# A two-layer gated cross-attention kernel: output weights split inside the first attention, semaphores cleared by runs, and a reordered merged stage

## The chip, the cores and the metric

The kernel runs on one core of a Trainium2 chip. The metric is the device time in microseconds (us) of one execution. A core has five engines that run their own programs and wait for each other by semaphores: PE (TensorE, matmuls; PEld is its weight load), DVE (VectorE), ACT (ScalarE), POOL (GpSimd) and SP (SyncE, which issues most transfers here).

## The reference

`x` is 2048 tokens of 512 numbers, `ctx_2048` as many. Two layers follow each other, and each adds two gated parts to `x`:

```
x = x + tanh(g_xattn[0]) * L0_xattn(layernorm(x), ctx)     # 16 heads of 128; in groups of 128 tokens
x = x + tanh(g_ffn[0])   * L0_ffn(layernorm(x))            # 8 experts, the best 2 of each token, and a shared one
x = x + tanh(g_xattn[1]) * L1_xattn(layernorm(x), ctx)     # 16 heads of 32; per token, over its own heads
x = x + tanh(g_ffn[1])   * L1_ffn(layernorm(x))            # weights rounded to -1, 0, 1 times their mean magnitude

L0_xattn: q, k = rms_norm(x @ q_w + q_b), rms_norm(ctx @ ki_w + ki_b); v = ctx @ vi_w + vi_b
          softmax(q k^T / sqrt(128)) v, then @ o_w + o_b
L1_xattn: Q, K, V = x @ Wq.T + bq, ctx @ Wk.T + bk, ctx @ Wv.T + bv
          score = einsum('bshd,bsgd->bshg', Q, K); softmax over g; einsum('bshg,bsgd->bshd') @ Wo.T + bo
```

## The kernel before

**Stages.** Four stages run one after the other: `l0_attention`, `l0_experts`, `l1_attention` (called the merged stage: it adds the experts' rows to x, and does the second attention) and `l1_output_ffn`. `build` wraps each in a call of `stage`: after the stage's own programs it clears on POOL, one instruction for one semaphore, the semaphores of the stage before it, and then meets all engines at a barrier. After the last stage the last semaphores are cleared in the same way.

**Precision.** Every 32-bit operand of a matmul is split in two: a high part (rounded to PE's fp32r by ACT, functions `..._high_part`) and a low part (operand minus high part, by POOL or DVE, `..._low_part`, `w_low`, `c_low`). A product takes three passes (`PASSES`), so 12 matmuls of 512 columns fill one 128x512 tile from a depth of 512.

**`l0_attention`.** The 2048 tokens go in four blocks of 512, each with 4 tiles of 128 tokens; the first three blocks are a hardware loop, the fourth is written out. A block takes 16 weight groups of 1 MB (`i` from 0 to 15) through two slots, `i % 2`: 4 for k, 1 for v, 4 for q, 3 more for v, and 4 for the output (from `O0` = 12). For each group SP loads (`load_w`), ACT rounds (`w_high_part`), POOL subtracts (`w_low`, one instruction of 128x2048), PE multiplies (`project`, `project_out`), and DVE takes the results (`take`). Beside groups 0 to 3 a tile of x is loaded (`load_x`), normalised on DVE and POOL (`normalise_x`), turned on PE (`turn_h`) and split (`h_high_part`, `h_low_part`). On each engine the written order is the order of execution. DVE's program for group `i` is: normalise tile `i`, then take the four results of group `i`. Inside group 11 all engines run `attention`: 16 units `u` of four heads and 128 tokens, scores, maximum, exponent, sum (`L631`) and reciprocal (`L633`), product on POOL (`L301`), turning with a lag of 3 units and weighing with a lag of 4. From unit 10 on ACT and DVE also split the first four heads for the output projection (`a_high_part`, `a_low_part`, `L612`). The weights of group 13 (the second of the output) are split after the attention. At a block's end DVE adds the bias to four residual tiles (`L664`), SP stores them (`L232`), and then loads x of the next block (`L202`).

**`l1_attention`.** Again four blocks `b` of 512 tokens. Its projections come as items (kind, block, tile): `h` turns a tile of normalised x, `k`, `v`, `q` are projections of 12 matmuls. The items of block 0 and `k` of block 1 come first, alone. Then 32 pairs `p` follow, 8 to a block (`w = p % 8`); each does a part of the attention of block `b` and holds two items of the next block, or of `k` of the block after that, in its two slots. Results of q, k, v are stored in DRAM and loaded again in another layout (`store`, `load_q`, `load_k`, `load_v`); ACT's `move_queries` lays q out before a block's first scores. In pairs 4 and 5 of blocks 0 and 1 the context of two blocks later is rounded (`c_high_part`) and subtracted (`c_low`), and in pairs 4 to 7 a tile of it is normalised (`tile_stats`, `power`, `tile_normalise`), whose expert rows POOL gathers (`gather`) two tiles ahead. The magnitudes of the last stage's weights are summed in 32 pieces (`sum_piece`, loads by `load_piece`), two in each of the last 16 pairs.

## Time and profile before

| what | us |
|---|---|
| median of 3 timed runs | 2105.95 (2105.8 to 2112.45) |
| the profiled execution, its device time | 2103.36 |
| the profiled execution, its span from the first to the last instruction | 2101.6 |
| PE busy in the span | 1928.2 (92%) |

The trace is of one execution. Its device time is 1.8 us more than its span. TensorE's mean granted clock is 0.966 of full speed. "Busy" of PE counts a matmul's modelled length, so it says where PE waited, and not that it was at its peak where it did not.

### The profile page before, as it was taken

To read this page: it belongs to the slowest core of one execution; us is meant where nothing else is said; L and a number is where in the kernel's file an instruction comes from. 1 tells how busy PE (TensorE), PEld (TensorE's weight loads), DVE (VectorE), ACT (ScalarE), POOL (GpSimd) and SP (SyncE) were. 2 spreads that over 40 slices of the span, in tenths; PEclk is the share of its full clock that TensorE was granted. 3 is DMA by queue.
4 is the path that set the end of the run, shared out by engine and by line. 5 is a ranking of instruction groups with operands and counts; after the bars stand their busy time and mean duration, and the time that the engine had idled before them with its cause. 6 is when DMAs were issued, how large, how long until landed. Compare 5 with 4: busy or idle time off the path is not lost. (4 is left out here: it accounts for less than half of the span.)

```text
span 2101.6 us, 29461 instructions
## 1 busy us (share of the span) xinstructions
PE 1928.2 (92%) x10300; PEld 1613.6 (77%) x10300; DVE 1039.0 (49%) x1659; ACT 749.7 (36%) x1128; POOL 1076.1 (51%) x807
## 2 busy tenths in 40 slices
PE   6999999999999999979999799998789875899997
PEld 5888788877897788857777699996677763678885
DVE  2547654765565655663341233334677764782111
ACT  3326333633345333622122112223333444443332
POOL 5765477547844775443227846523354323843332
PEclk9999999999999999989999899998999986999998
DMA  4231332224221322243217655423966555430000
GB/s 146 101 110 34 133 105 90 71 76 134 92 95 66 122 99 100 102 172 120 105 59 265 195 169 173 144 71 116 289 155 181 152 156 165 156 110 31 20 20 20
DMA packets 172236, 248.11 MB, mean 118 GB/s; under 512 B 44944, under 2 KB 69520, under 8 KB 172112
## 3 DMA queue, kind: packets, MB, share of 16 engines
q1 hardware_dynamic: 157024, 202.09, 30.7%
q0 software_dynamic: 9472, 34.09, 4.8%
q10 hardware_dynamic: 5616, 10.23, 1.3%
q8 instruction: 85, 1.39, 0.3%
q14 instruction: 39, 0.32, 0.1%
HBM read 179.77 MB, written 66.58 MB: 117 GB/s over the span
## 5 line engine op out<-in xcount | busy, mean ns | idle before, releaser
L255 POOL TENSOR_TENSOR a_w_hl<-a_w_raw,a_w_hl 128x2048 fp32r<-128x2048 f32 x63 | 290.7, 4615 | 150.8 <-ACT a_w_hl L320 150.8
L436 PE MATMUL a_proj<-a_c_hl,a_w_hl 128*128 128x512 f32 x768 | 183.0, 398 | 21.4 <-DVE a_w_hl L556 19.9
L436 PEld LDWEIGHTS a_proj<-a_c_hl,a_w_hl 128*128 128x128 f32 x768 | 146.1, 192 | 53.4 <-issue 20.3
L510 PE MATMUL a_proj<-a_w_hl,a_a_hl 128*128 128x512 f32 x768 | 179.5, 392 | 4.0 <-DVE a_a_hl L612 4.0
L436 PE MATMUL a_proj<-a_w_hl,a_c_hl 128*128 128x512 f32 x768 | 181.2, 392 | 0.0
L436 PE MATMUL a_proj<-a_a_hl,a_w_hl 128*128 128x512 f32 x768 | 176.4, 390 | 0.0
L320 ACT ACTIVATE a_w_hl<-a_w_raw 128x2048 fp32r<-128x2048 f32 x64 | 122.4, 1912 | 151.1 <-PE a_proj L436 106.7
L339 ACT ACTIVATE a_sq<-a_proj,a_vecs 128x512 f32<-128x512 f32 x128 | 88.0, 690 | 230.9 <-PE a_proj L436 153.4
L510 PEld LDWEIGHTS a_proj<-a_w_hl,a_a_hl 128*128 128x128 f32 x768 | 142.7, 188 | 34.3 <-POOL a_w_hl L255 5.5
L436 PEld LDWEIGHTS a_proj<-a_a_hl,a_w_hl 128*128 128x128 f32 x768 | 143.6, 188 | 29.7
L279 POOL TENSOR_TENSOR a_ssum<-a_ssum,a_sq 128x512 f32<-128x512 f32 x112 | 145.4, 1298 | 37.1 <-ACT a_sq L339 32.4
L436 PEld LDWEIGHTS a_proj<-a_w_hl,a_c_hl 128*128 128x128 f32 x768 | 142.4, 188 | 28.6
L1293 PE MATMUL b_gate_up<-b_wts,b_xt_hl 128*128 x936 | 159.8, 326 | 4.2 <-DVE b_xt_hl L1502 4.2
L2499 POOL TENSOR_TENSOR f_a_hl<-f_act_sb,f_a_hl 128x512 fp32r<-128x512 f32 x64 | 86.8, 1358 | 146.7 <-ACT f_a_hl L2547 146.6
L1293 PEld LDWEIGHTS b_gate_up<-b_wts,b_xt_hl 128*128 128x128 f32 x936 | 154.9, 191 | 8.2 <-issue 5.0
L612 DVE SCALAR_TENSOR_TENSOR a_a_hl<-a_qT,a_vecs,a_a_hl 128x512 fp32r<-128x512 f32 x64 | 101.1, 1609 | 81.7 <-ACT a_a_hl L353 81.7
L1199 PE MATMUL b_gate_up<-b_wts 128*128 128x512 f32 (+1 forms) x576 | 136.0, 394 | 0.0
L1896 POOL TENSOR_TENSOR p_probs<-p_own_sc,p_mask 128x512 f32<-128x512 f32 x64 | 67.8, 1082 | 128.9 <-DVE p_own_sc L2237 128.6
L1199 PEld LDWEIGHTS b_gate_up<-b_wts 128*128 128x128 f32 (+1 forms) x576 | 102.9, 179 | 29.4
L2607 PE MATMUL f_totals<-f_ternary,f_a_hl 128*128 128x512 f32 x512 | 122.6, 396 | 0.3 <-DVE f_ternary L2631 0.3
L2593 PE MATMUL f_hidden<-f_h_hl,f_ternary 128*128 x512 | 118.8, 389 | 0.0
L2607 PEld LDWEIGHTS f_totals<-f_ternary,f_a_hl 128*128 128x128 f32 x512 | 96.3, 188 | 23.9 <-issue 0.8
(254 smaller groups left out, 3522.7 us busy)
## 6 DMA issues: line engine op xcount, KB each, us to landing
a_w_raw<-in_a_ki_w SPq DMA_DIRECT2D x16, 1024.0 KB, 5.0
a_w_raw<-in_a_vi_w SPq DMA_DIRECT2D x16, 1024.0 KB, 4.9
a_w_raw<-in_a_q_w SPq DMA_DIRECT2D x16, 1024.0 KB, 4.9
a_w_raw<-in_a_o_w SPq DMA_DIRECT2D x16, 1024.0 KB, 5.3
spare<-in_b_gate_up POOLq DMA_DIRECT2D x32, 352.0 KB, 3.8
l_sorted_rows<-b_zeros SPq DMA_DIRECT2D x39, 256.0 KB, 3.2
spare<-l_sorted_rows SPq DMA_DIRECT2D x39, 256.0 KB, 3.2
l_expert_out<-spare ACTq DMA_DIRECT2D x39, 256.0 KB, 3.5
```

What stands on the lines that cost most here:

```text
L255: pool.tensor_tensor(w_hl[:, s, 1], w_raw[:, s], f32(w_hl[:, s, 0]), ALU.subtract)\
L279: pool.tensor_tensor(ssum[:], first, sq[:, n % 2, :], ALU.add).then_inc(sq_added, 1)
L320: act.activation(w_hl[:, i % 2, 0], w_raw[:, i % 2], ACT.Copy).then_inc(w_high, 1)
L339: act.activation(sq[:, n % 2, :], proj[:, j, :], ACT.Square, bias=bias)\
L436: mm = pe.matmul(proj[:, j, :], left, right, start=(k == 0 and n == 0), stop=(k == KC - 1 and n == 2))
L510: mm = pe.matmul(proj[:, j, :], a_hl[:, ap, k, j * P:(j + 1) * P], w_hl[:, i % 2, wp, k], start=(n == 0 and m == 0), stop=(n == 4 * G - 1 ...
L612: dve.scalar_tensor_tensor(a_hl[:, 1, n % 4, :], qT[:, n, :], v_b[:, n:n + 1], f32(a_hl[:, 0, n % 4, :]), ALU.add, ALU.subtract).then_inc( ...
L1199: mm = pe.matmul(gu_ps[0:w, n, part, :], gu_hl[:, s, wp, k, cols], h_hl[:, hslot, ap, k, :], start=(k == 0 and m == 0), stop=(k == KC - 1 ...
L1293: mm = pe.matmul(gu_ps[:, i % 2, half, 0:F], x_part(i, xp)[:, own], part(r, P, at, F), start=(k == 0 and xp == 0 and start == HI), stop=(k ...
L2499: pool.tensor_tensor(a_hl[:, 1, m % FC, :], act_sb[:, m % 2, :], f32(a_hl[:, 0, m % FC, :]), ALU.subtract).then_inc(g_split, 1)
L2593: mm = pe.matmul(h_ps[:, m % 2, :], w_t[:, 2 * g, k, f * P:(f + 1) * P], h_hl[:, ap, k, bass.ds(BLK * t, BLK)], start=(k == 0 and ap == 0) ...
L2607: mm = pe.matmul(y_ps[:, j, :], a_hl[:, ap, f, j * P:(j + 1) * P], w_t[:, 2 * g + 1, f, :], start=(m == 0 and ap == 0), stop=(m == NG * FC ...
```

## The change

Three parts of the program change.

1. In `l0_attention`, POOL's subtraction of a weight group is four instructions of 128x512 in place of one of 128x2048, everywhere. Group 13 is split inside the attention: ACT rounds a quarter in units 4, 5, 6 and 8 (`O_HIGH`), POOL subtracts a quarter in units 9, 10, 12 and 13 (`O_LOW`). Two of the four early `a_low_part` go behind the attention's loop. Tile 0 of x is turned and split together with tile 1, after group 1, and SP loads tiles 2 and 3 one group later.
2. In `build`, semaphores with numbers next to each other are cleared by one instruction.
3. In `l1_attention`, the expert rows of the first four tiles are gathered at once, two of them into buffers that are free until later; POOL subtracts the q weights and DVE the v weights (it was the other way round); `take_v` comes earlier in DVE's program; q is loaded before v in block 0. In the pairs, ACT's two roundings and POOL's two subtractions of the context come first in the pair. For the last block the items are h, h | h, h | q, q | q, q | v | v | v | v over the 8 pairs (they were h, v four times, then q, q twice, then none). The pieces are summed from pair 0 on, one in a pair (two in pairs 22 to 25), all on ACT, and are done after pair 27.

The diff, cut to its core:

```diff
+    O_HIGH, O_LOW = (4, 5, 6, 8), (9, 10, 12, 13)
...
-                    if i < 2:
-                        load_x(i + 2)
+                    if 0 < i < 3:
+                        load_x(i + 1)
...
             def w_low(n, i):
                 pool.wait_ge(w_high, n + 1)
                 s = i % 2
-                pool.tensor_tensor(w_hl[:, s, 1], w_raw[:, s], f32(w_hl[:, s, 0]), ALU.subtract)\
-                    .then_inc(w_split, 1)
+                for k in range(KC):
+                    ins = pool.tensor_tensor(w_hl[:, s, 1, k], w_raw[:, s, k], f32(w_hl[:, s, 0, k]), ALU.subtract)
+                ins.then_inc(w_split, 1)
...
                             if u % 4 == 3 and not last:
                                 c_low(KC * t + KC, u // 4)
-                        w_low(NW * t + i + 2, i + 2)
+                            if u in O_LOW:
+                                w_low_part(NW * t + i + 2, i + 2, O_LOW.index(u))
...
+                            if u in O_HIGH:
+                                act.wait_ge(proj_ready, NP * t + NP)
+                                w_high_quarter(NW // 2 * t + (O0 + 1) // 2 + 1, O0 + 1, O_HIGH.index(u))
...
-                    if i == O0:
-                        w_high_part(NW // 2 * t + (i + 1) // 2 + 1, (i + 1) % 2)
...
                     project(i)
-                    if i < TPB:
-                        turn_h(i)
+                    if 0 < i < TPB:
+                        for j in range(0 if i == 1 else i, i + 1):
+                            turn_h(j)
...
-                        if EARLY < u <= EARLY + 4:
+                        if EARLY < u <= EARLY + 2:
                             a_low_part(u - EARLY - 1)
+                    for n in (2, 3):
+                        a_low_part(n)
...
+    SLOTS = []
     for n in range(1, NBLK):
-        ITEMS += [(kind, n, j) for j in range(4) for kind in "hv"] + four("q", n)
+        pairs = list(zip(four("h", n), four("v", n)))
         if n + 1 < NBLK:
-            ITEMS += four("k", n + 1)
-    NI = len(ITEMS)
+            pairs += list(zip(four("q", n)[::2], four("q", n)[1::2])) + list(zip(four("k", n + 1)[::2], four("k", n + 1)[1::2]))
+        else:
+            pairs = list(zip(four("h", n)[::2], four("h", n)[1::2])) + list(zip(four("q", n)[::2], four("q", n)[1::2]))
+            pairs += [(item, None) for item in four("v", n)]
...
-        PIECES = []
-        for p in range(2 * NP, NP * NBLK):
-            PIECES += [(p, "act"), (p, "dve")] if p in (2 * NP + 4, 2 * NP + 5) else [(p, "act")] * 2
+        PIECES = [(p, "act") for p in range(28) for _ in range(2 if 22 <= p < 26 else 1)]
...
-            load_v(0)
             for j in range(TPB):
                 store("q", 0, j)
             load_q(0)
+            load_v(0)
...
+                if b + 2 < NBLK and w in (4, 5):
+                    c_low(b + 2, 2 * w - 8)
+                    c_low(b + 2, 2 * w - 7)
                 if p:
                     expand(2 * p - 2)
                     expand(2 * p - 1)
...
             tile_stats(0)
-            w_low("q", 0)
             tile_stats(1)
-            w_low("q", 1)
             tile_normalise(0)
-            tile_stats(2)
-            w_low("q", 2)
-            tile_normalise(1)
             dve.wait_ge(const_in, 32)
             take_v(0, 0)
+            tile_stats(2)
+            tile_normalise(1)
             take_v(0, 1)
...
+    def clear(sems):
+
+        numbers = sorted(s.num for s in sems)
+        first = [n for n in numbers if n - 1 not in numbers]
+        after = [n + 1 for n in numbers if n + 1 not in numbers]
+        for start, stop in zip(first, after):
+            nc.gpsimd.sem_clear(range(start, stop))
```

The order on PE at a block's start in `l0_attention` (written-out order of the first block; `a_proj` is the projection of a group, `a_turned` a turned tile of x). Before:

```order
L436 MATMUL a_proj<-a_c_hl,a_w_hl 128x512 x12
L445 MATMUL a_turned<-a_ident,a_xr 128x128 x4
L418 REGISTER_ALU
L430 ISA
L436 MATMUL a_proj<-a_c_hl,a_w_hl 128x512 x12
```

After:

```order
L455 MATMUL a_proj<-a_c_hl,a_w_hl 128x512 x12
L437 REGISTER_ALU
L449 ISA
L455 MATMUL a_proj<-a_c_hl,a_w_hl 128x512 x12
L449 REGISTER_ALU
L455 MATMUL a_proj<-a_c_hl,a_w_hl 128x512 x12
L449 REGISTER_ALU
L455 MATMUL a_proj<-a_c_hl,a_w_hl 128x512 x12
L449 REGISTER_ALU
L455 MATMUL a_proj<-a_c_hl,a_w_hl 128x512 x12
L464 MATMUL a_turned<-a_ident,a_xr 128x128 x8
```

Nothing stands between the last tile of group 0 and the first of group 1 any more, and both turned tiles come after group 1.

The order on POOL ahead of the attention, in it and behind it (`a_rq` is the reciprocal root for q, `a_probs` is the product of unit u, `a_c_hl` the context's subtraction, `a_w_hl` that of the weights), in the last block. Before:

```order
L255 TENSOR_TENSOR a_w_hl<-a_w_raw,a_w_hl 128x2048
L283 TENSOR_TENSOR a_rq<-a_rq,a_mhalf 128x4
L255 TENSOR_TENSOR a_w_hl<-a_w_raw,a_w_hl 128x2048 x2
L301 TENSOR_TENSOR a_probs<-a_probs,a_rden 128x512 x16
L255 TENSOR_TENSOR a_w_hl<-a_w_raw,a_w_hl 128x2048 x3
```

After:

```order
L292 TENSOR_TENSOR a_rq<-a_rq,a_mhalf 128x4
L257 TENSOR_TENSOR a_w_hl<-a_w_raw,a_w_hl 128x512 x8
L310 TENSOR_TENSOR a_probs<-a_probs,a_rden 128x512 x10
L263 TENSOR_TENSOR a_w_hl<-a_w_raw,a_w_hl 128x512
L310 TENSOR_TENSOR a_probs<-a_probs,a_rden 128x512
L263 TENSOR_TENSOR a_w_hl<-a_w_raw,a_w_hl 128x512
L310 TENSOR_TENSOR a_probs<-a_probs,a_rden 128x512 x2
L263 TENSOR_TENSOR a_w_hl<-a_w_raw,a_w_hl 128x512
L310 TENSOR_TENSOR a_probs<-a_probs,a_rden 128x512
L263 TENSOR_TENSOR a_w_hl<-a_w_raw,a_w_hl 128x512
L310 TENSOR_TENSOR a_probs<-a_probs,a_rden 128x512 x2
L257 TENSOR_TENSOR a_w_hl<-a_w_raw,a_w_hl 128x512 x8
```

The subtraction of group 13 is in the attention now, and the other two are eight shorter instructions.

The order on POOL in pairs 4 and 5 of the merged stage (`p_probs` is `expand`, `p_c_hl` is `c_low`, `p_rstd` is `power`, the DMA is `gather`). Before:

```order
L1896 TENSOR_TENSOR p_probs<-p_own_sc,p_mask 128x512 x8
L1877 TENSOR_TENSOR p_c_hl<-carry,p_c_hl 128x512
L1883 TENSOR_TENSOR p_rstd<-p_rstd,p_mhalf 128x1
L1877 TENSOR_TENSOR p_c_hl<-carry,p_c_hl 128x512
L1871 DMA p_routed<-l_expert_out,place 128x512 x2
L1896 TENSOR_TENSOR p_probs<-p_own_sc,p_mask 128x512 x2
L1877 TENSOR_TENSOR p_c_hl<-carry,p_c_hl 128x512
```

After:

```order
L1931 TENSOR_TENSOR p_probs<-p_own_sc,p_mask 128x512 x6
L1912 TENSOR_TENSOR p_c_hl<-carry,p_c_hl 128x512 x2
L1931 TENSOR_TENSOR p_probs<-p_own_sc,p_mask 128x512 x2
L1918 TENSOR_TENSOR p_rstd<-p_rstd,p_mhalf 128x1
L1906 DMA p_routed<-l_expert_out,place 128x512 x2
L1912 TENSOR_TENSOR p_c_hl<-carry,p_c_hl 128x512 x2
L1931 TENSOR_TENSOR p_probs<-p_own_sc,p_mask 128x512 x2
```

The two subtractions of a pair stand ahead of its expansions, and `power` no longer stands between them. By the same listing POOL's clears are 59, 86 and 68 after the second, third and fourth stage and 44 at the end before, and 1, 1, 1 and 4 after.

## Rows read from the trace of the kernel before

**Rows 1.** Stretches of `l0_attention` and of the merged stage: length, busy (instructions), clock, DMA.

```profile
core 0: us, PE busy (x) PEld busy (x) DVE busy (x) ACT busy (x) POOL busy (x), PEclk, DMA share, GB/s
0.00:917.90 917.90, 869.86 (x4512) 738.35 (x4512) 516.71 (x703) 378.56 (x482) 555.01 (x294) 1.00 0.29 98
...
1449.80:1781.30 331.50, 265.60 (x1920) 213.94 (x1920) 224.47 (x437) 138.58 (x253) 131.97 (x128) 0.88 0.67 185
```

**Rows 2.** One line's instructions: the clears after the third stage; ns, first and last start.

```profile
L2729 POOLq EVENT_SEMAPHORE_RANGE_CLEAR  x86: 37/38/38, 1775.5 to 1781.0; - x86
```

**Rows 3.** Timeline of PE, start of block 1 in `l0_attention`: start, length, [idle before, releaser].

```profile
242.22 11.17 PE L436 MATMUL a_proj<-a_c_hl,a_w_hl 128*128 128x512 f32 x48 [0.53 <-DVE a_xr L661]
256.08 0.66 PE L445 MATMUL a_turned<-a_ident,a_xr 128*128 128x128 f32 x4 [2.70 <-DVE a_xr L569]
256.81 12.82 PE L436 MATMUL a_proj<-a_c_hl,a_w_hl 128*128 128x512 f32 x48
```

**Rows 4.** Waits of PE up to 917 us: us in total, times, longest.

```profile
PE a_turned L445 <- DVE a_xr L569: 8.3, 3, 3.1
PE a_turned L485 <- POOL a_probs L301: 8.0, 12, 1.3
PE a_proj L510 <- DVE a_a_hl L612: 4.0, 4, 1.0
```

**Rows 5.** Timeline of all engines at the same block start; last, line L664 alone.

```profile
243.72 4.68 POOL L255 TENSOR_TENSOR a_w_hl<-a_w_raw,a_w_hl 128x2048 fp32r<-128x2048 f32 x1 [6.19 <-ACT a_w_hl L320]
...
244.63 4.32 DVE L664 TENSOR_TENSOR a_sq<-a_sq,a_tg_ob 128x512 f32<-128x512 f32 x1
...
250.01 0.90 SPq L202 DMA_DIRECT2D a_xr<-in_x  x2
...
255.95 2.96 DVE L587 TENSOR_SCALAR spare<-a_proj,a_vecs,a_nqk 128x512 f32<-128x512 f32 x4
...
L664 DVE TENSOR_TENSOR a_sq<-a_sq,a_tg_ob x8: 691/692/4320, 243.2 to 914.4; 128x512 f32<-128x512 f32 x8
```

**Rows 6.** Costliest groups (busy, mean ns); then lines L2470 and L2636: ns min/median/max.

```profile
L255 POOL TENSOR_TENSOR a_w_hl<-a_w_raw,a_w_hl 128x2048 fp32r<-128x2048 f32 x63 | 290.7, 4615 | 150.8 <-ACT a_w_hl L320 150.8
L279 POOL TENSOR_TENSOR a_ssum<-a_ssum,a_sq 128x512 f32<-128x512 f32 x112 | 145.4, 1298 | 37.1 <-ACT a_sq L339 32.4
...
L2470 POOL TENSOR_TENSOR f_h_hl<-f_a_raw,f_h_hl x12: 1273/1296/1303, 1791.9 to 1824.2; 128x512 fp32r<-128x512 f32 x12
L2470 POOL TENSOR_TENSOR f_h_hl<-carry,f_h_hl x4: 1266/1718/1726, 1782.1 to 1786.7; 128x512 fp32r<-128x512 f32 x4
...
L2636 DVE TENSOR_TENSOR f_a_hl<-carry,f_a_hl x4: 1345/1760/1768, 1782.5 to 1787.2; 128x512 fp32r<-128x512 f32 x4
```

**Rows 7.** Timeline behind the first attention; last, line L612 alone.

```profile
203.48 4.61 POOL L255 TENSOR_TENSOR a_w_hl<-a_w_raw,a_w_hl 128x2048 fp32r<-128x2048 f32 x1 [7.17 <-ACT a_w_hl L320]
...
208.78 32.91 PE L510 MATMUL a_proj<-a_w_hl,a_a_hl 128*128 128x512 f32 x144 [0.97 <-DVE a_a_hl L612]
...
L612 DVE SCALAR_TENSOR_TENSOR a_a_hl<-a_qT,a_vecs,a_a_hl x64: 719/740/4602, 181.5 to 901.4; 128x512 fp32r<-128x512 f32 x64
```

**Rows 8.** Timeline of PE, start of the merged stage (items v2 and v3).

```profile
1476.80 7.09 PE L2092 MATMUL p_proj<-p_w_hl,p_c_hl 128*128 128x512 f32 x24 [3.89 <-DVE p_outs L2197]
```

**Rows 9.** Timeline, pair 6 of the merged stage; last, that wait over the whole stage.

```profile
1562.26 1.50 POOL L1877 TENSOR_TENSOR p_c_hl<-carry,p_c_hl 128x512 fp32r<-128x512 f32 x1
...
1563.91 5.11 PE L2092 MATMUL p_proj<-p_c_hl,p_w_hl 128*128 128x512 f32 x12 [5.71 <-POOL p_c_hl L1877]
...
PE p_proj L2092 <- POOL p_c_hl L1877: 11.4, 2, 5.7
```

**Rows 10.** Timeline of PE, first pair of the merged stage's last block.

```profile
1715.87 2.08 PE L2107 MATMUL p_scores<-p_k,carry 32*128 32x128 f32 x16 [8.29 <-ACT carry L1981]
```

**Rows 11.** Timeline, pairs 30 to 33 of the merged stage.

```profile
1747.09 1.94 PE L2116 MATMUL p_turned<-p_ident,p_probs 128*128 128x128 f32 x8 [2.01 <-ACT p_probs L1995]
...
1756.66 0.63 ACT L1986 ACTIVATE p_w_piece<-p_w_piece 128x512 f32<-128x512 f32 x1 [8.54 <-DMA p_w_piece<-in_w_ffn]
...
1758.62 1.94 PE L2116 MATMUL p_turned<-p_ident,p_probs 128*128 128x128 f32 x8 [5.73 <-ACT p_probs L1995]
```

More of the change, by code:

```diff
@@ L642, in block_of_tokens @@
                             take(i, j)
-                    if i < TPB:
-                        h_low_part(i)
+                    if 0 < i < TPB:
+                        for j in range(0 if i == 1 else i, i + 1):
+                            h_low_part(j)
                     if i == AT["v", 0]:
@@ L1630, in l1_attention @@
         x_in = [sem(f"x_in{j}") for j in range(TPB)]
-        got = [sem(f"got{s}") for s in range(2)]
+        got = [sem(f"got{s}") for s in range(TPB)]
         first_added = sem("first_added")
@@ L1803, in _ @@
                 load_x(2, j)
+            for m in range(2):
+                load_piece(m)
             for p in range(NP * NBLK):
@@ L1849, in _ @@
                         sp.dma_start(y_next[:, j, :], x2[j * P:(j + 1) * P, :]).then_inc(next_in, 16)
-                if p == PIECES[0][0] - 2:
-                    for m in range(2):
-                        load_piece(m)
                 for m in pieces_beside(p):
@@ L2727, in stage @@
         run(nc, new_sem, *args)
-        for s in used:
-            nc.gpsimd.sem_clear(s)
+        clear(used)
         nc.all_engine_barrier()
@@ L2746, in build @@
                 stage(l1_output_ffn, x2, aT, part("d_"), a["w_ffn"], sums, carry[:], out)
-    for s in used:
-        nc.gpsimd.sem_clear(s)
+    clear(used)
     last[0].close()
```

93 lines of the change are left out of this document (56 added, 37 removed).

## The prediction

> **What bounds the kernel now.** I read the stretches by stage first, then the waits of PE, then the timeline around each long wait. In `l0_attention` PE is busy for 869.9 of 917.9 us, in the merged stage for 265.6 of 331.5 us [rows 1]. The reader sees that PE is the bound where it has its data, so time can be won only at its waits, and after a wait the matmuls also run slower for some microseconds: 48 matmuls take 11.17 us before the wait and 12.82 us after it [rows 3]; at the merged stage's granted clock of 0.88 [rows 1], part of the stretch is at 1.2 GHz and not at 2.4.
>
> **The change part by part.** The terms are made against the profiled execution (2103.36 us). The median of the timed runs, 2105.95, stands 2.6 us above it.
>
> *Clears.* 86 clears start between 1775.5 and 1781.0: 0.065 us each [rows 2]. They stand between two stages, or at the very end, where every other engine waits. The listing has 59 + 86 + 68 + 44 = 257 of them before and 7 after: 250 x 0.065 = **16.0 us**. No row shows a clear of a long run of numbers. Bounds: 0 (it costs as much as the single ones) and 16.2. I take 16.0, since the instruction of before is already one on a range and takes 38 ns.
>
> *Block starts of `l0_attention`.* Three of the four blocks start with the same chain. POOL's subtraction starts at 243.72 for 4.68 us; DVE's last bias addition (L664), issued at 244.63, lasts 4.32 us, where it takes 0.69 alone [rows 5]. SP stores its result and only then loads x (250.01); normalising tile 0 stands ahead of DVE's first take, which comes at 255.95 [rows 5]. PE waits for the tile (2.70 us), and could not have started group 1 either, since that needs the first take. So moving `turn_h` alone wins nothing; what wins is the subtraction in quarters. Where POOL and DVE both do such subtractions they alternate: 1.72 us and 1.76 us each, against 1.30 us for POOL alone [rows 6]. A first quarter would end at 243.72 + 1.30 = 245.0, L664 at 245.7, 3.2 us sooner than 248.95. The load goes to 246.8 and the first take to 252.7, 0.7 us before PE ends group 0 at 242.22 + 11.17 = 253.4. So both waits go: 8.3 us over the three blocks [rows 4] and the slower matmuls of one, 12.82 - 11.17 = 1.65 us [rows 3]: **10.0 us**. Bounds 0 and 11.
>
> The Trainium skill (SBUF — State Buffer, "Who interferes with whom") says that GpSimd and a VectorE operation with two SBUF inputs exclude each other for a whole instruction, and the later one waits in full. By that rule, the 4.32 us agree. It doesn't say who is served between two GpSimd instructions that follow at once; if POOL kept its turn, this term would be 0, which is a rival below.
>
> *What the quarters cost.* Four quarters take 4 x 1.30 = 5.2 us, not 4.61 [rows 6]. In a group of k or q POOL also adds four squares of 1.30 us: 10.4 us together, under PE's 11.17 us for a group. PE's work hides it: 0.
>
> *Group 13 in the attention.* Now PE waits 4.0 us in four blocks [rows 4]: the subtraction that starts at 203.48 holds back DVE's L612, and PE starts at 208.78 after 0.97 us of idle [rows 7]. With the subtraction done earlier, ACT and DVE have only the activations to split: **3.9 us**. ACT gets four quarters of the rounding and POOL four of 1.30 us in units 4 to 13.
>
> *End of the attention.* PE waits 8.0 us for POOL's product there, 2.0 a block [rows 4], since DVE's four early L612 of 0.72 us [rows 7] lengthen a chain that otherwise keeps PE's pace. Two leave it: 1.44 us a block. Against it, POOL has product and quarter in four units, and a quarter in flight can hold back each of the two L612 that stay by up to 1.3 us. I take half of the gain lost and a little more: 0.65 x 4 = **2.6 us**. Bounds: -4 (every hold-back in full) and +8.
>
> *Start of the merged stage.* PE waits 3.89 us for `take_v`, behind DVE's wait for expert rows, and its next 24 matmuls take 7.09 us [rows 8], against half of 11.17 = 5.6. Rows gathered at once and `take_v` moved up remove both, 3.89 + 1.5 = 5.4; the first `power` now stands behind eight gathers on POOL, so I take **4.6 us**. Bounds 0 and 5.4.
>
> *Context first in a pair.* PE waits 5.71 us for the last of POOL's subtractions (1562.26 + 1.50) and runs the next 12 matmuls in 5.11 us, not 2.8; the wait comes twice, 11.4 us [rows 9]. In the new order the roundings fall where ACT waits for PE anyway, and the last subtraction no longer waits for the second item of pair 5, but for the start of that pair, 12 matmuls and more earlier. 11.4 + 2 x 2.3 = 16; I take **15.5 us**. The expansions of those pairs come up to 2 x 1.50 = 3 us later; they are used a pair later, so that costs 0. Bounds 11.4 and 16.
>
> *Order of the last block's items.* PE waits 8.29 us for `move_queries` of the last block [rows 10]. q is now projected two pairs earlier, and its round trip through DRAM is over in time. But the move (on ACT) still comes behind pair 23's exponent, so PE waits for the rest of a pair's chain on DVE; and the block's first two pairs now hold transposes only, so that DVE sets their pace, and q waits there for the last split. No row prices these two; I take **3.4 us**, a little under the middle between the bounds 0 and 8.3, because both losses are sure in kind.
>
> *Pieces early.* In the last block ACT waits up to 8.54 us for a piece, since SP has twelve loads for the next stage in the same queue, and PE waits 2.01 and 5.73 us for ACT's copies behind it [rows 11]. The new kernel has no piece left in its last four pairs. 7.7 us and 0.8 us for the slower instructions around: **8.5 us**. Bounds 4 and 10. In exchange SP waits in each earlier pair for ACT's sum; the stores behind that wait have a pair or more of slack: 0.
>
> Sum: 16.0 + 10.0 + 3.9 + 2.6 + 4.6 + 15.5 + 3.4 + 8.5 = 64.5 us. 2103.36 - 64.5 = 2038.9 for a profiled run, and with the 2.6 us a median of **2041 us**.
>
> **The rivals.**
> - *DVE isn't served between quarters.* Then the block starts give 0 and the end of the attention loses 4: 16.6 us less, 2058 us. For it: the four quarters follow each other at once. Against it: the even 1.72 and 1.76 us [rows 6]. Chance 0.12.
> - *A long clear costs what its single ones did.* 16 us less: 2057 us. No row speaks for it. Chance 0.06.
> - *SP's queue.* `load_piece` waits at each pair's end for ACT; q, k and v stand behind it. If the loads of a block came as late as q does now, PE would wait some 8.3 us [rows 10] at each of three block changes: 25 us less, 2066 us. Against it: those loads are issued two pairs before they are used. Chance 0.08.
> - *POOL becomes the bound of `l0_attention` (slower).* A group of k or q leaves a quarter (11.17 - 5.2) / 4 = 1.5 us. If DVE's instructions came between them so that a quarter took 2.1 us, each of 8 groups in 4 blocks would be 2.4 us late: 77 us, 2118 us. It decides from 2.0 us a quarter. Against it: in the projections DVE reads PSUM for nearly all its work, and POOL's 4.61 us show no hold-up there. Chance 0.03.
> - That what is won at one wait is lost at the next, so that nothing is left (within 0.3%): 0.01.
>
> **How the numbers follow.** My forecast has 0.70. Its own range: the eight terms' distances to their bounds, taken together as independent, are about 11 us: 2030 to 2052. To hold 8 in 10 the range must take in the two cases at 2057 and 2058 and leaves the others out: **2028 to 2060**. 0.3% is 6.3 us, about what a measurement of this kernel tells from no change. Faster by more than that: the first four cases, 0.96; within it 0.01; slower 0.03.
>
> **What the profile of the changed kernel would show.** Right: one clear between stages, and four at the end, with the next stage's first instruction within 0.2 us of it; L664 (now with a quarter beside it) at 1.1 us or less and not 4.32, and no idle of PE before group 1; no idle before the second output group; no wait of PE for the context in pairs 6 and 14; ACT without a wait for pieces after pair 27. Wrong: L664 still over 4 us; the wait of PE for POOL's product grown past 8 us; new idle of PE before q of the last block over 2 us, or before a block's first scores; POOL busy without a gap in the groups of k and q.

## The result

| what | before | changed |
|---|---|---|
| median, us | 2109.2 (2105.8 to 2114.39, 4 runs) | 2049.49 (2047.59 to 2050.89, 4 runs) |
| profiled execution, device time / span, us | 2103.36 / 2101.6 | 2048.61 / 2046.8 |

The ratio is 0.972, with a 95% interval of 0.9696 to 0.9744: faster. 2041 us were predicted, with a range of 2028 to 2060. The spans of the two profiled executions differ by 54.8 us, where the terms sum to 64.5. The medians are 59.7 us apart: the profiled execution of before, 2103.36 us, is a quick one, and its median was 2106.45 to 2109.2 in four sets of runs. The account by stages below rests on that one profile, so its terms may be some us low in sum. The changed kernel again, in a later set of runs, took 2048.12 us.

### The profile page after: what moved, and what is told of

Read it like the earlier page. It is cut to its first block and busy times, and to the rows that moved or that the text cites. A ratio compares the mean times of both kernels' runs of the same rounds, so it can differ in the third digit from the quotient of the medians.

```text
span 2046.8 us, 29418 instructions
## 1 busy us (share of the span) xinstructions
PE 1918.5 (94%) x10300; PEld 1608.7 (79%) x10300; DVE 987.4 (48%) x1657; ACT 752.6 (37%) x1144; POOL 1114.2 (54%) x996
## 5 line engine op out<-in xcount | busy, mean ns | idle before, releaser
L257 POOL TENSOR_TENSOR a_w_hl<-a_w_raw,a_w_hl 128x512 fp32r<-128x512 f32 x236 | 312.7, 1357 | 142.9 <-ACT a_w_hl L330 142.7
L455 PE MATMUL a_proj<-a_c_hl,a_w_hl 128*128 128x512 f32 x768 | 179.8, 394 | 21.8 <-DVE a_w_hl L576 19.9
L330 ACT ACTIVATE a_w_hl<-a_w_raw 128x2048 fp32r<-128x2048 f32 x60 | 114.8, 1914 | 152.0 <-PE a_proj L455 106.7
L632 DVE SCALAR_TENSOR_TENSOR a_a_hl<-a_qT,a_vecs,a_a_hl 128x512 fp32r<-128x512 f32 x64 | 67.4, 1068 | 96.3 <-ACT a_a_hl L370 96.3
```

The lines of the kernel that those rows point to most:

```text
L257: ins = pool.tensor_tensor(w_hl[:, s, 1, k], w_raw[:, s, k], f32(w_hl[:, s, 0, k]), ALU.subtract)
L330: act.activation(w_hl[:, i % 2, 0], w_raw[:, i % 2], ACT.Copy).then_inc(w_high, 1)
L455: mm = pe.matmul(proj[:, j, :], left, right, start=(k == 0 and n == 0), stop=(k == KC - 1 and n == 2))
```

## The profile of the changed kernel, beside that of before

The windows of the two stages that [rows 1] showed, here in the changed kernel:

```profile
core 0: us, PE busy (x) PEld busy (x) DVE busy (x) ACT busy (x) POOL busy (x), PEclk, DMA share, GB/s
0.00:897.77 897.77, 865.28 (x4512) 737.13 (x4512) 460.28 (x703) 379.63 (x494) 596.06 (x484) 1.00 0.29 101
1426.95:1731.69 304.74, 258.56 (x1920) 208.94 (x1920) 228.74 (x435) 140.36 (x257) 129.88 (x129) 0.93 0.73 202
```

`l0_attention` is 20.2 us shorter, the merged stage, with the clears at its end, 26.8 us. PE is busy for 4.6 and 7.0 us less with the same matmuls, since fewer of them run slowly behind a wait.

**`l0_attention`.** The waits of PE in this stage (the 19.9 us are the start of the kernel, in both alike):

```profile
PE a_proj L455 <- DVE a_w_hl L576: 19.9, 1, 19.9
PE a_turned L504 <- POOL a_probs L310: 4.0, 8, 0.7
PE a_proj L455 <- DVE spare L607: 1.8, 3, 0.9
```

Against [rows 4] the waits for tile 0 and for the second output group are gone, and the wait for POOL's product is halved. What is left at a block's start is 0.6 us a block, for DVE's first take. The timeline of the first block change (us from the start, length, then idle before it and what ended it):

```profile
240.44 5.55 POOL L257 TENSOR_TENSOR a_w_hl<-a_w_raw,a_w_hl 128x512 fp32r<-128x512 f32 x4 [5.33 <-ACT a_w_hl L330]
...
241.34 1.00 DVE L687 TENSOR_TENSOR a_sq<-a_sq,a_tg_ob 128x512 f32<-128x512 f32 x1
...
243.40 0.91 SPq L203 DMA_DIRECT2D a_xr<-in_x  x2
...
247.88 1.50 DVE L589 TENSOR_SCALAR a_xr<-a_xr,a_mv,a_rstd 128x512 f32<-128x512 f32 x1 [0.67 <-POOL a_rstd L298]
...
249.30 2.96 DVE L607 TENSOR_SCALAR spare<-a_proj,a_vecs,a_nqk 128x512 f32<-128x512 f32 x4
...
250.16 11.19 PE L455 MATMUL a_proj<-a_c_hl,a_w_hl 128*128 128x512 f32 x48 [0.87 <-DVE spare L607]
```

The last bias addition, 4.32 us in [rows 5], takes 1.00: it ends 0.6 us after 241.74, where a first quarter of 1.30 us ends. So DVE gets its turn between two quarters here, which the forecast had to assume. The Trainium skill (SBUF — State Buffer, "Who interferes with whom") has the later of the two wait for a whole instruction; the trace agrees. It adds that DVE can be let in between instructions that follow at once, but the merged stage shows a place where it isn't (below, at "Context first in a pair").

**Clears.** Seven of them, in place of 257:

```profile
L2755 POOLq EVENT_SEMAPHORE_RANGE_CLEAR  x7: 44/239/502, 1426.3 to 2046.6; - x7
```

A long one takes up to 502 ns, where one that cleared one semaphore took 38. From the last work of a stage to the next one's first instruction (at the end, to the span's end):

| place | before | changed | won | semaphores |
|---|---|---|---|---|
| ahead of the merged stage | 6.57 | 3.15 | 3.42 | 59 |
| ahead of the last stage | 12.39 | 7.42 | 4.97 | 86 |
| at the end | 10.29 | 3.68 | 6.61 | 68 + 44 |

15.0 us in all, 0.058 us for each semaphore.

**The merged stage.** PE's waits in it:

```profile
PE p_scores L2140 <- issue: 11.1, 3, 4.3
...
PE p_proj L2125 <- DVE p_c_hl L2191: 7.5, 2, 6.8
PE p_scores L2140 <- ACT carry L2014: 6.7, 1, 6.7
PE p_scores L2140 <- DVE p_masked_sc L2248: 5.9, 5, 1.2
PE p_turned L2149 <- POOL p_probs L1931: 3.4, 4, 1.8
PE p_proj L2125 <- DVE p_a_hl L2223: 2.7, 1, 2.7
```

The waits for the context's low part in pairs 6 and 14 [rows 9] and for the pieces [rows 11] don't appear any more. New is the first line: PE waits 4.21, 4.34 and 2.53 us ahead of the scores of pairs 8, 16 and 24. Pair by pair, from the starts of `scores` in the timeline (us; "first" is from the stage's first instruction to the first scores, "end" from the last scores to the next stage's first instruction):

| kernel | first | pairs 0-6 | 7 | 8-14 | 15 | 16-23 | 24-30 | end |
|---|---|---|---|---|---|---|---|---|
| before | 65.88 | 57.86 | 10.80 | 60.81 | 10.80 | 59.89 | 34.95 | 30.51 |
| changed | 64.04 | 50.98 | 12.97 | 52.94 | 13.10 | 57.63 | 32.98 | 20.10 |
| changed, again | 64.89 | 50.63 | 13.40 | 54.23 | 13.10 | 60.32 | 31.23 | 20.62 |
| `e1_clears` | 66.59 | 59.21 | 10.80 | 61.10 | 10.80 | 60.26 | 34.86 | 25.40 |
| `e4_context` | 65.99 | 50.01 | 12.77 | 54.49 | 12.85 | 59.83 | 34.86 | 30.29 |
| `e7_order` | 62.91 | 50.05 | 13.43 | 54.10 | 13.11 | 59.97 | 31.95 | 20.08 |
| `e8_pieces_late` | 63.73 | 50.74 | 12.76 | 52.92 | 12.86 | 66.55 | 33.65 | 25.04 |
| `e5_move` | 61.27 | 50.57 | 9.33 | 53.29 | 9.98 | 59.31 | 33.71 | 20.08 |

The first two rows give the account of this stage: 1.8 us sooner at the first scores (0.9 of it given back in pair 0), 15.7 us in the two stretches that held the context waits (pair 0 left out), 4.5 us lost in pairs 7 and 15, and 9.7 us won from pair 16 on when the 5.0 us of the clears are taken off the end. Pair 0 takes 6.7 to 7.6 us in kernels with the old start and 6.6 to 7.7 in those with the new one, so the 0.9 us may be chance. That is 21.8 us without the clears, where 32.0 were predicted (4.6, 15.5, 3.4 and 8.5).

The rest of the difference of the spans is in code that the change doesn't touch: the experts' stage between its first matmul and its last result took 0.7 us longer, the last stage 1.5 us.

## The experiments

Times are medians; the ratio is to the kernel before in the same set of runs (2106.45 us for the first four kernels, 2108.52 for the next four, 2108.31 for the last four).

### One part alone

**Clears.** The kernel before with `clear` in place of the single clears:

```diff
-        for s in used:
-            nc.gpsimd.sem_clear(s)
+        clear(used)
```

> The kernel before, with the clears by runs alone. The three places where clears stand (ahead of the merged stage, ahead of the last stage, at the end) became 3.4, 5.0 and 6.6 us shorter in the changed kernel. Theory: these 15.0 us belong to the clears alone, so this kernel is 15 us faster, with the stages themselves as before. Rival: a part of it came from what ends each stage in the changed kernel (the transfers that SP waits for there); then under 12 us.

2090.79 us, ratio 0.9936 (0.9911 to 0.996): 13.5 us by the ratio, with an interval of 8.4 to 18.7; the medians are 15.7 us apart. The gaps decide more closely than the whole time. The three gaps are 3.15 us (1442.09 to 1445.24), 7.39 us (ahead of the last stage) and 3.7 us at the end (2085.34 to 2089.0), the same as in the changed kernel. The term stands at 15 us.

**Quarters.** The kernel before with this alone:

```diff
-                pool.tensor_tensor(w_hl[:, s, 1], w_raw[:, s], f32(w_hl[:, s, 0]), ALU.subtract)\
-                    .then_inc(w_split, 1)
+                for k in range(KC):
+                    ins = pool.tensor_tensor(w_hl[:, s, 1, k], w_raw[:, s, k], f32(w_hl[:, s, 0, k]), ALU.subtract)
+                ins.then_inc(w_split, 1)
```

> The kernel before, with POOL's subtraction of a weight group in four instructions alone; tiles are turned and loaded as before, group 13 is split after the attention. Theory of the prediction: DVE is served between two quarters, so the last bias addition of a block takes about 1.1 us and not 4.32, the three waits for tile 0 (8.3 us) go, and the four waits of 1.0 us at the second output group shrink too, since what is in DVE's way is 1.3 us and not 4.6: 10 to 13 us faster. Rival: the tile would be in time only because it is turned a group later; then the wait for it stays at 2 us or more a block, and under 5 us are won.

2101.26 us, ratio 0.9977 (0.9967 to 0.9987): 4.8 us by the ratio, 5.2 by the medians, where 10 to 13 were expected. The waits of PE in `l0_attention`:

```profile
PE a_proj L444 <- DVE a_w_hl L564: 20.0, 1, 20.0
PE a_proj L518 <- POOL a_w_hl L256: 8.4, 4, 2.1
PE a_turned L493 <- POOL a_probs L309: 8.0, 12, 1.3
PE a_turned L453 <- DVE a_xr L577: 0.6, 1, 0.6
```

The waits for tile 0 fell from 8.3 to 0.6 us with the tiles turned as before, so it is the quarters that remove them, and turning tile 0 later is worth next to nothing. But at the second output group a wait of 2.1 us a block came where 1.0 was: four quarters take longer than one instruction, and there DVE and POOL alternate, and the last quarter is what PE now waits for.

**Group 13 in the attention.** The complement of it, the kernel before with the quarters of group 13 alone (in units of the attention, as in the changed kernel), and the two early parts behind the loop:

```diff
+                            if u in O_LOW:
+                                w_low_part(NW * t + i + 2, i + 2, O_LOW.index(u))
...
-                        if EARLY < u <= EARLY + 4:
+                        if EARLY < u <= EARLY + 2:
```

> The kernel before, with group 13 split inside the attention (quarters for this group alone) and two of the four early parts behind the loop; all other groups in one subtraction, tiles turned as before. Theory: l0_attention's gain has two independent halves. This half removes the four waits at the second output group (4.0 us) and half of the wait for POOL's product (8.0 to 4.0 us) and leaves the three waits for tile 0 at 8.3 us: 8 to 9 us faster. Rival: without quarters everywhere, POOL's other subtractions still hold DVE back at the attention's end, so that PE's wait for the product stays at 8 us; then 4 us are won.

2098.91 us, ratio 0.9962 (0.995 to 0.9975): 8.0 us by the ratio. The waits in the stage:

```profile
PE a_turned L462 <- DVE a_xr L586: 9.0, 3, 3.1
PE a_turned L502 <- POOL a_probs L309: 4.0, 8, 0.7
PE a_proj L453 <- DVE a_xr L680: 0.7, 2, 0.3
```

As expected, the wait at the second output group is gone, the one for the product halved, the one for tile 0 untouched. The rival falls.

**All of `l0_attention`.**

The edits of part 1 of the change, and no other.

> The kernel before, with every edit of l0_attention (quarters, group 13 inside the attention, tile 0 turned with tile 1, two early parts moved). Theory: this stage is the same program as in the changed kernel, so it ends 20.2 us sooner, and nothing of it is given back later: 20 us faster. Rival: the gain in the changed kernel came in part from elsewhere; then 16.5 us, as the prediction's terms for this stage sum to.

2087.28 us, ratio 0.9914 (0.9896 to 0.9933), 18.1 us by the ratio; the stage ends at 899.17 us, 18.8 us sooner than in the profile of before. The interval leaves room for both figures of the expectation, 20 and 16.5. The two halves alone sum to 4.8 + 8.0 = 12.8 us, and together they give 18.1. Most of the difference is the second output group: the quarters alone raise its waits from 4.0 to 8.4 us, and with group 13 inside the attention these 4.4 us don't arise.

**Context first in a pair.** The kernel before with:

```diff
+                    if b + 2 < NBLK and w in (4, 5):
+                        c_high_part(b + 2, 2 * w - 8)
+                        c_high_part(b + 2, 2 * w - 7)
                     item_part(2 * p)
```

and the same on POOL.

> The kernel before, with the context's roundings and subtractions first in their pair alone; pieces, items and the start as before. Both context waits should go (15.7 us over pairs 6 and 14). Theory: these waits also let DVE get ahead; without them the exponent of pairs 7 and 15 comes later, ACT's move of the queries behind it too, and PE waits 4.2 us ahead of the scores of pairs 8 and 16 where it waited 2.04: 11 us faster in all. Rival: the longer waits there come from the pieces, which in the changed kernel are loaded and summed in these pairs; then they stay at 2.04 here, and 15.5 us are won.

2097.49 us, ratio 0.9964 (0.9952 to 0.9976), 7.6 us by the ratio, 9.0 by the medians. From the first scores to those of pair 16, 130.12 us took 10.15 us less than the 140.27 of before. Both context waits went, and pairs 7 and 15 each take 2 us more, with no piece near them. The timeline at pair 8:

```profile
1576.17 0.60 DVE L2226 TENSOR_TENSOR p_own_sc<-p_own_sc,p_mx 128x128 f32<-128x128 f32 x1
1576.81 0.31 ACT L1989 ACTIVATE p_own_sc<-p_own_sc 128x128 f32<-128x128 f32 x1 [2.72 <-DVE p_own_sc L2226]
1577.02 0.58 ACT L2002 ACTIVATE p_o<-p_out 128x512 f32<-128x512 f32 x1
1577.50 1.18 ACT L1955 ACTIVATE p_outs<-p_proj,p_bias 128x512 f32<-128x512 f32 x1
1578.46 1.93 ACT L1979 ACTIVATE carry<-carry 128x2048 f32<-128x2048 f32 x1
1580.49 1.88 PE L2105 MATMUL p_scores<-p_k,carry 32*128 32x128 f32 x16 [4.01 <-issue]
```

ACT is idle for 2.72 us until DVE has subtracted the maximum; only then come the exponent, a copy, k's take and the move of the queries (the row of `carry`), and PE waits for the move. In the kernel before, at the same place:

```profile
1579.82 0.31 ACT L1991 ACTIVATE p_own_sc<-p_own_sc 128x128 f32<-128x128 f32 x1
...
1581.37 1.19 ACT L1957 ACTIVATE p_outs<-p_proj,p_bias 128x512 f32<-128x512 f32 x1 [0.76 <-PE p_proj L2092]
...
1582.35 1.92 ACT L1981 ACTIVATE carry<-carry 128x2048 f32<-128x2048 f32 x1
...
1584.37 1.16 PE L2107 MATMUL p_scores<-p_k,carry 32*128 32x128 f32 x16 [2.04 <-issue]
```

There the exponent had no wait, since in PE's 5.71 us [rows 9] DVE had caught up, and ACT's next wait was for PE.

How far DVE is behind shows in the time from a pair's scores on PE to DVE's first masked scores of the same pair. In pairs 4, 5, 6 and 7 it is 1.2, 4.8, 6.9 and 1.2 us in the kernel before, 1.2, 2.3, 5.0 and 4.7 us in the changed one, and 1.2, 2.1, 4.8 and 4.5 us in this one. In block 1 the first two kernels have the same numbers within 0.25 us. The kernel before at pair 7:

```profile
1573.57 1.16 PE L2107 MATMUL p_scores<-p_k,carry 32*128 32x128 f32 x16
1574.80 0.69 DVE L2215 TENSOR_TENSOR p_masked_sc<-p_scores,p_mask 128x512 f32<-128x512 f32 x1 [2.38 <-PE p_scores L2107]
```

The changed kernel from pair 5 to pair 7:

```profile
1528.83 3.18 POOL L1912 TENSOR_TENSOR p_c_hl<-carry,p_c_hl 128x512 fp32r<-128x512 f32 x2
1528.85 3.32 DVE L2270 TENSOR_TENSOR p_own_sc<-p_own_sc,p_rden 128x128 f32<-128x128 f32 x1
...
1538.31 0.68 DVE L2248 TENSOR_TENSOR p_masked_sc<-p_scores,p_mask 128x512 f32<-128x512 f32 x1
...
1541.97 1.16 PE L2140 MATMUL p_scores<-p_k,carry 32*128 32x128 f32 x16
...
1546.66 0.68 DVE L2248 TENSOR_TENSOR p_masked_sc<-p_scores,p_mask 128x512 f32<-128x512 f32 x1
```

POOL's two subtractions of the context put DVE behind. A short DVE instruction, 0.29 us elsewhere, is issued 0.02 us after the first of them and ends 0.16 us after the second: it lasts 3.32 us, so DVE isn't let in between the two. Every kernel with the context first has this instruction at 3.29 to 3.35 us in pairs 5 and 13; in the kernel before it never lasts over 0.30. Once behind, DVE gains little: its round from 1538.31 to 1546.66 takes 8.35 us, PE's pair 8.70. In the kernel before DVE fell behind at the same subtractions too, since `power` stood between them and DVE waited for it, and PE's wait for them let it catch up. In the new order PE no longer waits for them, but DVE still does. Without this one hold the exponent would come 3.0 us sooner, which is what ACT waits for it (2.72 us here, 2.91 and 3.06 in the changed kernel); that is an estimate from these rows, and no run keeps the two subtractions apart.

The windows of pairs 4 to 6, from scores to scores, say the same more roughly. First the kernel before, then the changed one:

```profile
1539.66:1573.57 33.91, 28.20 (x195) 22.69 (x193) 25.06 (x47) 13.23 (x21) 19.42 (x19) 0.90 0.55 155
```

```profile
1515.88:1541.97 26.09, 26.09 (x195) 21.07 (x193) 23.25 (x40) 14.27 (x25) 17.16 (x16) 1.00 0.65 176
```

DVE (the third busy time, after PE and PEld) is busy for 25.06 of 33.91 us before, 74%, and for 23.25 of 26.09 us after, 89%. The windows don't hold the same work, 47 and 40 of its instructions, since DVE is behind at the end of the second one, and the time for which POOL holds it counts as busy, 3.0 us of it in the one instruction above.

### One part undone in the changed kernel

**Pieces late.** `PIECES` and the loads of the first two pieces as before:

```diff
-        PIECES = [(p, "act") for p in range(28) for _ in range(2 if 22 <= p < 26 else 1)]
+        PIECES = []
+        for p in range(2 * NP, NP * NBLK):
+            PIECES += [(p, "act"), (p, "dve")] if p in (2 * NP + 4, 2 * NP + 5) else [(p, "act")] * 2
```

> The changed kernel, with the pieces summed as before (two in each of the last 16 pairs, two of them on DVE). Theory: the stage's end from pair 24 on took 53.1 us before and 45.7 in the changed kernel, all of it by the pieces: 7.4 us slower, and the waits ahead of pairs 8 and 16 stay at 4.2 us. Rival: the pieces' loads and SP's waits for their sums in pairs 0 to 15 cause those two waits; then they fall to 2.0 us and the loss is under 4 us.

2058.36 us, ratio 0.9759 (0.9739 to 0.9778), 8.2 us slower than the changed kernel by the ratios. The waits ahead of pairs 8 and 16 stay at 4.00 and 4.10 us, so neither the pieces nor SP's waits for them cause those. From pair 24 on the stage takes 5.6 us more, less than 7.4; another 8.9 us are in pairs 16 to 23, of which 2.7 may be chance, by the two profiles of the changed kernel (57.63 and 60.32). These sum to more than the 8.2 us of the timed runs, because the profile is of the slowest of the four executions, 3.2 us above their median. PE waits 3.7 us for DVE's masked scores ahead of pair 23; the changed kernel has no wait there, and the kernel before 0.9 us. So the new order of items and the late pieces seem to harm each other; no other run has the two together.

**Order of the last block's items.**

```diff
         else:
-            pairs = list(zip(four("h", n)[::2], four("h", n)[1::2])) + list(zip(four("q", n)[::2], four("q", n)[1::2]))
-            pairs += [(item, None) for item in four("v", n)]
+            pairs += list(zip(four("q", n)[::2], four("q", n)[1::2])) + [(None, None)] * 2
```

> The changed kernel, with the last block's items in the order of the kernel before (h, v four times, q, q twice, then none). Pairs 16 to 24 took 59.9 us before and 57.6 in the changed kernel. Theory: this 2.3 us is what the order gives, since the wait ahead of pair 24 shrinks by 5.8 us and the two pairs with transposes alone give back 2.70 us at the first q and about 0.8 us in DVE's pace. Undone, this kernel is 2 us slower in pairs 16 to 24, and again waits some 8 us ahead of pair 24; v's items move out of pairs 20 to 23, where they are PE's only ones, which changes nothing in the sum. Rival: the pieces carry a part of it; then undoing the order costs 4 us or more, or nothing.

2049.68 us, ratio 0.9717 (0.9698 to 0.9736), no difference from the changed kernel that the timing shows. The wait ahead of pair 24 is 6.80 us again, not 2.53. Pairs 16 to 23 take 59.97 us, against 57.63 and 60.32 in the two profiles of the changed kernel, and pairs 24 to 30 take 31.95, against 32.98 and 31.23. So the 2.3 us of the first pair of profiles is no more than what one and the same program varies by, and the theory isn't shown. Over pairs 16 to 30 together it is 91.9 us here, against 90.6 and 91.6 in the changed kernel and 90.5 in `e6_v_first`, which has the new order too: 0.4 to 1.4 us for the order once the pieces are early, by one profile with the old order.

**v before q at the start.**

```diff
+            load_v(0)
             for j in range(TPB):
                 store("q", 0, j)
             load_q(0)
-            load_v(0)
```

> The changed kernel, with v of block 0 loaded before q is stored and loaded, as in the kernel before. In the changed kernel the queries of block 0 are there 10.2 us after the issue of their load, 8.5 us in the kernel before, and PE waits 6.67 and 4.77 us for them ahead of the first scores. Theory: v's 1 MB, issued right behind q's, takes a share of the DMA engines from it; with v first the load takes about 8.5 us again and the wait shrinks by 1.7 us. Rival: the gathers and the stores of x beside it set the load's time; then the wait stays at 6.7 us. Second rival: v's load holds q's stores back on SP; then the wait grows by 1 us or more. The first scores' time within the stage decides, since the whole time can't show 1.7 us.

2049.66 us, ratio 0.9727 (0.97 to 0.9753). PE waits 7.3 us for the queries. They take 7.9 us from the issue of their load to the move (1478.12 to 1486.00), where they took 10.2 in the first profile of the changed kernel and 8.1 to 10.4 in the others with this start. But SP issues the load 54.6 us after the stage's start and not at 50.2 to 52.4, since q's stores now land behind v's load:

```profile
1466.43 0.37 SPq L1799 DMA_DIRECT2D p_v<-l_vT  x1
1466.86 3.62 SPq L1772 DMA_DIRECT2D l_qT<-p_outs  x4
1478.12 1.94 SPq L1786 DMA_DIRECT2D carry<-l_qT  x4
```

So v's 1 MB delays either q's way out to DRAM or, perhaps, its way back. The second rival has the mechanism, but not quite the size: the wait is 0.6 us longer than in the first profile of the changed kernel and 1.3 us longer than in the second (6.00 us). The first scores come 64.50 us after the stage's start, within the 61.18 to 64.89 of the other place, so no run shows that one place is better.

### A fix for the new wait

**The move ahead of the exponents.**

```diff
                 if p < NP * NBLK:
+                    if b + 1 < NBLK and w == 7:
+                        move_queries(b + 1)
                     exponents(p)
...
-                    if b + 1 < NBLK and w == 7:
-                        move_queries(b + 1)
```

> The changed kernel, with ACT's move of the queries ahead of the exponents of the last pair of a block, and not behind them and the pair's second item. Theory: PE's waits ahead of the scores of pairs 8, 16 and 24 (4.21, 4.34 and 2.53 us) come from the place of the move on ACT, behind an exponent that waits for DVE; ACT has 2.9 us idle ahead of that exponent and the move takes 1.9 us. The waits go, and the slower matmuls behind two of them (about 1.7 us each): 11 to 15 us faster than the changed kernel. Rival: the queries themselves come late from DRAM (their load is issued 9 us before PE wants them, and took 8.5 and 10.2 us in block 0); then the move waits for them and holds the exponent back, and under 5 us are won.

2042.14 us, ratio 0.9687 (0.9667 to 0.9706). Ahead of pair 8:

```profile
1545.68 1.91 ACT L2014 ACTIVATE carry<-carry 128x2048 f32<-128x2048 f32 x1 [0.95 <-DMA carry<-l_qT]
...
1547.64 0.31 ACT L2024 ACTIVATE p_own_sc<-p_own_sc 128x128 f32<-128x128 f32 x1
...
1547.69 1.16 PE L2140 MATMUL p_scores<-p_k,carry 32*128 32x128 f32 x16 [0.57 <-issue]
```

The 4.21 us are 0.57 (1.44 in the second profile of this kernel, `e11_move_again`), so it was the move's place that PE waited for. Two things hold the gain under the 11 us of the theory; the first is a part of what the rival says. The move now waits 0.95 and 1.60 us for the queries from DRAM. And PE, 7 us ahead, runs into DVE: behind pair 16 it waits 2.21 us for the masked scores, then 1.17 and 1.88 us for splits. Pairs 7 and 15 give 3.6 and 3.1 us; 16 to 23 give 1.7 us back against the first profile of the changed kernel, and nothing against the second.

Both kernels side by side, unchanged, with more rounds:

> The same kernel as e5_move, on the chip on which the changed kernel runs again, to have the two beside each other. Theory: the gain of 7 us is real: the medians differ by 6 to 8 us. Rival: half of it was the first scores' time, which differs from run to run (61.3 to 64.5 us after the stage's start in programs that are alike up to there); then they differ by 3 to 5 us.

> The changed kernel again. Theory: 2049 to 2050 us, l0_attention ends at 898 us and the first scores come 61 to 65 us after the merged stage's start. Rival to the reading of the start's term (0.9 us in the first profile, up to the fourth row of scores): that this profile was typical, and not a late one; then the first scores come at 64 us again.

2041.39 us (0.9682, 0.9667 to 0.9697) against 2048.12 us (0.9719, 0.9702 to 0.9735): 6.7 us between the medians, and the intervals don't meet. The changed kernel's first scores come at 64.89 us, so its first profile (64.04) was not a late one. Over all profiles they came at these times: 62.91, 63.73, 64.04 and 64.89 in kernels with the changed start, but 61.27, 61.18 and 62.24 in those with the earlier move, which is the same program up to there; 65.14 to 67.75 in the six with the old start. So the start gives 66.3 - 62.9 = 3.4 us by the means, or 2.4 us by the four without the earlier move (63.9), and why the kernels with the earlier move come first among them isn't settled. The theory of the 6 to 8 us holds for the timed runs, but between the two profiles 3.7 us of the difference lie ahead of the first scores (2.3 us by the means), where the programs are alike. How much the move itself gives isn't settled closer than this: at pairs 7 and 15 it is 6.7 us in the first pair of profiles and 5.9 in the second.

**With the old order too.**

The edits of `e5_move` and `e7_order` in one kernel.

> The changed kernel with the earlier move of the queries, and the last block's items in the old order too. With the earlier move alone pairs 16 to 24 took 59.3 us and the rest of the stage 53.8 us, since DVE enters block 3 late and the transposes of the first two pairs wait for its splits (2.2, 1.2 and 1.9 us). Theory: spread over four pairs the transposes cost DVE less at once, so pairs 16 to 19 pass without these waits, and the whole is 1 to 4 us faster than with the move alone. Rival: q is then loaded two pairs later, the move stands ahead of the exponents and waits for it, and pair 23 to 24 costs 5 us or more instead.

2039.42 us, ratio 0.9677 (0.9662 to 0.9692), the lowest median of all, but its interval overlaps that of the move alone (0.9667 to 0.9697). Behind pair 16 the waits for DVE are gone, as expected; ahead of pair 24 PE waits 6.75 us for the move, as the rival says. The two nearly cancel.

## Why the prediction was right in sign and 8 us off in size

| term | predicted | measured | by |
|---|---|---|---|
| clears | 16.0 | 15.0 | three gaps, twice |
| block starts | 10.0 | 7.7 | waits, from 8.3 + 1.2 to 1.8 |
| group 13 | 3.9 | 4.0 | waits |
| end of the attention | 2.6 | 4.0 | waits, from 8.0 to 4.0 |
| slower matmuls of these three | in block starts | 4.6 | PE's busy time |
| start of the merged stage | 4.6 | 0.9; 3.4 by means | first scores |
| context first | 15.5 | 15.7 - 4.5 = 11.2 | stretches 0-6 to 15 |
| order and pieces | 11.9 | 9.7 | pair 16 to the end |

The measured terms sum to 57.1 us, and 2.2 us are lost in the two stages that don't change, which leaves 54.9, where the spans differ by 54.8. The forecast stood closer than its terms did, since `l0_attention` gave 3.8 us more than predicted and the merged stage 10.2 us less.

- **Clears**: right in kind. (250 x 0.065 is 16.2 and not 16.0, the bound and not the term.) The step that takes the new clear at the length of an old one was wrong, up to 502 and not 38 ns, and cost little, since there are seven and not 257. The rival (a long one costs what its single ones did) falls with `e1_clears`.
- **Block starts**: right. DVE is served between quarters (1.00 us), so the rival of 16.6 us falls, for this place. "0.7 us before PE ends group 0" didn't come true: the first take comes too late for PE, which still waits 0.6 us a block.
- **What the quarters cost: 0**. Right for k and q groups, wrong at one place if taken by itself: at the second output group they raise the waits from 4.0 to 8.4 us. It costs nothing in the changed kernel only because group 13 is split earlier. The sum came out because both edits were made.
- **End of the attention**: 4.0 us, half of the wait, and not 2.6. The hold-back by quarters that the forecast took off the gain was priced too high.
- **Slower matmuls**: only 1.65 us were counted in this stage, PE's busy time fell by 4.6 [rows 1]. With the waits that is 7.7 + 4.0 + 4.0 + 4.6 = 20.3 us in place of 16.5, the 20.2 of the windows.
- **Context first in a pair**: here the prediction failed. The wait and its price were right (15.7 us in two stretches). What wasn't asked is who else is held by POOL's subtractions, and what else had used PE's wait. The two subtractions stand next to each other now and hold DVE for 3.0 us, as one long subtraction did at the block starts; the prediction had this mechanism and didn't look for it here. DVE, which needs 8.35 us for a pair of 8.70, could catch up only in PE's wait. Without it the exponent of the block's last pair waits 2.7 to 3.1 us for DVE, the move of the queries stands behind it, and PE waits 4.2 us where it waited 2.0. The text named "new idle before a block's first scores" as what would make it wrong, and had the very chain ("the move still comes behind pair 23's exponent") for the last block, but not for the two others. `e4_context` shows it alone, `e8_pieces_late` shows that the pieces have no part in it, and `e5_move` that the move's place is what PE waits for. That the hold is what makes DVE late is read from the timelines; no run undoes the hold alone.
- **SP's queue**: the rival's mechanism isn't there. PE does wait more at the first two block changes, by 2.2 and 2.3 us, but for ACT, and it waits as long with the pieces late (4.00 and 4.10 us).
- **Start of the merged stage**: the waits at v are gone, as forecast (PE ends k of block 1 57.4 us after the stage's start, 61.1 before), but the trip of q through DRAM ends last there: PE waits 6.67 us for it and not 4.77. The step left out is the same: PE comes sooner to a wait whose end it doesn't set. How much of that wait a run has depends on the transfer (8.1 to 10.4 us over the profiles with this start).
- **Order of the items**: 3.4 us taken between 0 and 8.3; by the profiles 0.4 to 1.4, and by the timed runs not told from 0. Both losses named there came (2.70 us for the last split, DVE's pace) and eat the gain.
- **Pieces early**: 8.5 us predicted. Old order and late pieces take 59.8 + 34.9 + 25.3 = 120.0 us from pair 16 on (`e4_context`, 5.0 us of clears taken off), old order and early pieces 112.0 (`e7_order`): 8.0 us, by one profile each.
- **Range**: the "about 11 us" come out only if the lower bounds of the clears (16 us away) and of the block starts (10 us) are left to the rivals; with all eight terms it would be 22 us.
- **Signs**: two of those named as wrong came true, new idle before a block's first scores, and 2.70 us before q of the last block. Two of those named as right were missed by little: PE still idles up to 0.9 us before group 1, and the next stage's first instruction comes 0.3 us behind the clear.

## What to carry to other kernels

Before a wait on the critical engine is priced, look at who else is behind at that moment: an engine that needs nearly the whole of a round may use just this wait to catch up, and the next thing that stands behind it in a queue is late once the wait is gone. Ask also whether the work that the critical engine waited for holds up another engine too, and still does in the new order. A long GpSimd instruction cut into pieces can let VectorE in between them, but not at every place, and it is longer itself; look for the place where its end is waited for. "Busy" of VectorE includes the time for which GpSimd holds it. And a term of 2 or 3 us has to be read in two profiles of the same program before it is believed.

## What the runs showed of the hardware

- One clear of a run of semaphores took 44 to 502 ns in seven instructions that cleared 257 between them; single ones 37 to 47 ns each, and 0.065 us from one to the next.
- VectorE's addition of 128x512, issued in GpSimd's first of four back-to-back subtractions, took at most 1.00 us in any block, against 4.32 us beside one long subtraction.
- VectorE isn't always let in between GpSimd instructions that follow at once. A 128x128 operation of 0.29 us, issued 0.02 us after the first of two subtractions of 1.6 us, took 3.29 to 3.35 us, in pairs 5 and 13 of nine kernels. The same operation in pair 4, issued 0.3 to 1.2 us after the first one's start, took 0.64 to 1.49 us and ended 0.2 us after the first one (changed kernel, `e7_order`, `e12_changed_again`). What decides it isn't shown.
- The same load of 1 MB of queries from DRAM, in programs that are the same up to there, took 8.1 to 10.4 us from its issue until ACT could use it (seven profiles).
